# Routing of a mixture of experts inside an attention loop: its VectorE work moved between two other operations, its phases moved to other steps, shared batches started earlier

## The reference

```python
# x: (16, 256, 256), ctx: (16, 77, 256); 16 heads of 64
z = layernorm(x)
x = x + tanh(g_xattn) * cross_attention(keys_values=concat(LN(ctx), LN(z)), queries=LN(z)) @ Wo
h = layernorm(x)                       # 4096 rows of 256
logits = h @ router_w + router_bias    # 16 experts, the last one is the identity
top_w, top_i = top_k(softmax(logits), 2); w = top_w / sum
routed = w[15] * h + sum_e w[e] * (silu(h @ gate[e]) * (h @ up[e])) @ down[e]
shared = silu(causal_conv3(h)) * (h @ shared_up) @ shared_down
x = x + tanh(g_ffn) * (shared + routed)
```

## Time and profile before

| | |
|---|---|
| median of three runs | 1423.63 us (1422.02 to 1424.4) |
| profiled execution | 1424.07 us, its span 1422.3 us |
| busy: PE, DVE, ACT, POOL | 1267.8 (89%), 936.7 (66%), 636.0 (45%), 741.2 (52%) |
| mean granted TensorE clock | 0.984 |
| POOL per step | 0.74 us (L1094) and three times L1097 |

### The profile page before, as it was taken

One profiled execution on the slowest core, in us unless ns is written; L12 is line 12 of the kernel. 1 busy time (PEld: TensorE's weight loads), 2 busy tenths in 40 slices (PEclk: granted clock), 3 DMA queues, 4 the chain that ended last, 5 costly groups with the idle time before them and its releaser, 6 DMA issues.

```text
span 1422.3 us, 28174 instructions
## 1 busy us (share of the span) xinstructions
PE 1267.8 (89%) x8982; PEld 1020.6 (72%) x8982; DVE 936.7 (66%) x2710; ACT 636.0 (45%) x1956; POOL 741.2 (52%) x894
## 2 busy tenths in 40 slices
PE   1899999999998999899999998999999967998995
PEld 1677777777777777777777776777777755777774
DVE  4566676777776777677767776777776655445555
ACT  2554545454544454445444444444455412333332
POOL 1645546474656565556555655565554611444444
PEclk9999999999999999999999999999999989999998
DMA  4940000000000000000000000000000331335555
GB/s 129 310 122 4 3 1 18 1 19 1 18 1 20 2 18 8 13 6 14 9 13 9 11 9 13 9 11 9 9 12 5 94 104 41 105 118 167 177 171 189
DMA packets 61827, 70.94 MB, mean 50 GB/s; under 512 B 7056, under 2 KB 56160, under 8 KB 61664
## 3 DMA queue, kind: packets, MB, share of 16 engines
q1 hardware_dynamic: 54464, 49.96, 12.2%
q0 software_dynamic: 6912, 18.95, 3.6%
q10 hardware_dynamic: 288, 0.00, 0.0%
HBM read 35.19 MB, written 33.70 MB: 48 GB/s over the span
## 4 chain that ended last, share of the span: by engine, by line
PE 57%; DVE 21%; ACT 11%; issue 8%; DMA 2%; POOL 0%; DVEq 0%; SPq 0%; ACTq 0%; POOLq 0%
PE pj L1333 15%; PE st L1363 9%; ACT probs L1147 8%; PE st L1379 7%; PE ov L1398 5%; DVE neg_max L1286 5%; PE yb L1460 5%; PE st L539 4%; PE pj L492 3%; DVE OT_hl L1297 2%; PE ov L558 2%; ACT OT_hl L1155 1%; PE st L529 1%; DVE PT L1315 1%; PE ov L997 1%
## 5 line engine op out<-in xcount | busy, mean ns | idle before, releaser
L1097 POOL TENSOR_SCALAR probs<-probs,inv_sum 128x333 f32<-128x333 f32 x384 | 427.1, 1126 | 0.0
L1147 ACT ACTIVATE probs<-st,neg_max 128x333 f32<-128x333 f32 x512 | 268.8, 538 | 298.6 <-DVE neg_max L1286 298.6
L1094 POOL TENSOR_TENSOR probs<-probs,inv_sum 128x333 f32<-128x333 f32 x128 | 94.7, 740 | 457.0 <-DVE inv_sum L1293 457.0
L1286 DVE TENSOR_REDUCE neg_max<-st 128x2 f32<-128x666 f32 x256 | 205.9, 846 | 117.6 <-PE st L1379 115.0
L1363 PE MATMUL st<-ident,probs 128*128 128x128 f32 (+1 forms) x1536 | 206.7, 274 | 9.9 <-ACT probs L1147 9.9
L1363 PEld LDWEIGHTS st<-ident,probs 128*128 128x128 f32 (+1 forms) x1536 | 181.2, 145 | 28.9 <-ACT probs L1147 10.4
L1398 PE MATMUL ov<-PT,V 128*64 128x256 f32 (+1 forms) x1536 | 196.7, 391 | 0.1
L1333 PE MATMUL pj<-wkv,lT 128*128 128x512 f32 (+1 forms) x576 | 160.0, 414 | 28.8 <-DVE Q_hl L1302 28.6
L1315 DVE COPY PT<-st 128x512 f32<-128x512 f32 x256 | 164.3, 683 | 11.3 <-PE st L1363 9.8
L1379 PE MATMUL st<-K_hl,Q_hl 64*128 64x334 f32 x1536 | 153.1, 329 | 19.5 <-issue 8.0
L1379 PEld LDWEIGHTS st<-K_hl,Q_hl 64*128 64x128 f32 x1536 | 120.6, 187 | 41.5 <-issue 36.3
(11 more groups left out here) (175 smaller groups left out, 1815.3 us busy)
## 6 DMA issues: line engine op xcount, KB each, us to landing
slots_x<-zeros SPq DMA_DIRECT2D x10, 1032.0 KB, 13.2
V<-slots_x SPq DMA_DIRECT2D x80, 129.0 KB
yg<-routed_y SPq DMA_DIRECT2D x32, 256.0 KB, 3.1
out<-X SPq DMA_DIRECT2D x32, 128.0 KB
stage<-in_L_xattn_Wkv SPq DMA_DIRECT2D x4, 512.0 KB, 4.3
X<-in_x SPq DMA_DIRECT2D x2, 1024.0 KB, 14.6
w_gu<-in_L_ffn_expert_gate_w SPq DMA_DIRECT2D x2, 960.0 KB, 9.6
w_gu<-in_L_ffn_expert_up_w SPq DMA_DIRECT2D x2, 960.0 KB, 10.4
```

Source lines behind the costliest of these rows:

```text
L1094: pool.tensor_tensor(probs[:, v, 0, 0:SKV], probs[:, v, 0, 0:SKV], inv_sum[:, v, 0:1].to_broadcast([P, SKV]), ALU.mult).then_inc(normed, 1)
L1097: pool.tensor_scalar(probs[:, v, i, 0:SKV], probs[:, v, i, 0:SKV], inv_sum[:, v, i:i + 1], None, ALU.mult).then_inc(normed, 1)
L1147: nc.scalar.activation(probs[:, v, i, 0:SKV], st_bank(i)[:, 0:SKV], ACT.Exp, bias=neg_max[:, v, i:i + 1], accum_out=sums[:, v, i:i + 1]).t ...
L1286: nc.vector.tensor_reduce(neg_max[:, v, 2 * i:2 * i + 2], st[i][:, :, 0:SKV], AX.X, ALU.max, negate=True).then_inc(maxed, 1)
```

## The change

Routing phases get other steps and names: STATS 13, VAR 14, ROWS 16, TURN 17 and 18, LOGITS 19, PICK and RANK 22, PAGES 23, SLOTS (and the first scatter) 26, SECOND 27. So they fall on p = 5 (STATS), 6 (VAR, PICK, RANK), 7 (PAGES), 0 (ROWS), 1 and 2 (TURN), 2 (SLOTS), 3 (LOGITS, SECOND). `L_STEPS` moves from p = 3, 4 to 4, 5. On VectorE `route_vector` goes from the end of the step to the place between the maxima (and layer norm) and the reciprocal; `route_vector_reads` goes to the end. On TensorE `route_tensor` goes behind the transposes, ahead of the output projection; on ScalarE `route_scalar` goes to the end of the step.

Behind attention, the last steps of attention and routing (128 to 147) become items ("attend") of the written order, with nine shared items among them instead of seven, the first behind step 128. A shared item is split on VectorE: `shared` keeps the normalised rows of the batch after the next, `gate` has the rest and comes, among the tiles, one tile later. Shared items stand behind every eighth tile. The early `weights` cover 28 row tiles.

```diff
-    EARLY = 7
+    EARLY = 9
+    WEIGHED = QT * (B - 2)
...
+        steps = list(range(att.N, att.last_step + 1))
+        goes_along = (1, 1, 2, 1, 2, 2, 3, 4, 4)
         items = []
         for i in range(EARLY):
+            for _ in range(goes_along[i]):
+                items.append(("attend", steps.pop(0)))
+            if i == 2:
+                items.append(("weights", slice(0, WEIGHED)))
+            items += [("shared", i), ("gate", i)]
...
-            if i % 7 == 6 and shared < B + 2:
+            if i % 8 == 0 and EARLY + i // 8 == shared:
+                if i:
+                    items.append(("gate", shared - 1))
+            if i % 8 == 7 and shared < B + 2:
                 items.append(("shared", shared))
                 shared += 1
...
         def shared(i):
+            if i == 0:
+                dve.wait_ge(att.h_rows, B - 2)
+                rows(0)
+            if i + 1 < B:
+                rows(i + 1)
+
+        def gate(i):
             on = live(i, 3, B)
...
-    L_STEPS = {3: 0, 4: 1}
+    L_STEPS = {4: 0, 5: 1}
...
+    STATS, VAR, ROWS, TURN, LOGITS, PICK, RANK, PAGES, SLOTS, SECOND = 13, 14, 16, 17, 19, 22, 22, 23, 26, 27
...
@@ vector, step: between layer norm and the reciprocal
             if exists(b + 1) and exists(b) and p < 3:
                 layer_norm(b + 1, p)
+            route_vector(dve, bb, u, has)
             if has(LAG_S):
                 m, v = PAIRS * bb + u - LAG_S, (u - LAG_S) % 2
                 dve.wait_ge(exped, 4 * m + 4)
                 nc.vector.reciprocal(inv_sum[:, v, :], sums[:, v, :]).then_inc(inv_ready, 1)
...
-            route_vector_reads(dve, bb, u, has)
             next_rows = p in L_STEPS and exists(b + 1) and exists(b)
...
-            route_vector(dve, bb, u, has)
+            route_vector_reads(dve, bb, u, has)
...
@@ tensor, step: behind the transposes, ahead of the output projection
-            if (turns_conv or any(phase(bb, u, has, f) for f in (15, 16, 17, 19))) and has(LAG_AV):
-                pe.wait_ge(ot_lo, PAIRS * bb + u - LAG_AV + 1)
+            if has(LAG_Y):
+                pe.wait_ge(ot_lo, PAIRS * bb + u - LAG_Y + 1)
...
+            route_tensor(pe, bb, u, has)
             if has(LAG_Y):
```

More of the change, by code:

```diff
@@ L465, in combine, with tensor @@
                 add(t, 1).then_inc(final, 1)
-        follow(dve, att.route_vector, {"shared": shared, "weights": weights, "tile": tile, "sum": combine})
-    def tensor(pe):
+        follow(attend, {"shared": shared, "gate": gate, "weights": weights, "tile": tile, "sum": combine})
+    def tensor(pe, attend):
         for i, free in enumerate(att.pj_free):
@@ L716, in attention @@
     cv_full = sem("cv_full")
-    route_in = {f: sem(f"route_in{f}") for f in (12, 17, 18, 20, 21, 22)}
-    CHAIN = {12: 1, 17: 2, 18: 4, 20: 7, 21: 7, 22: 1}
+    STATS, VAR, ROWS, TURN, LOGITS, PICK, RANK, PAGES, SLOTS, SECOND = 13, 14, 16, 17, 19, 22, 22, 23, 26, 27
+    route_in = {f: sem(f"route_in{f}") for f in (STATS, LOGITS, PICK, PAGES, SLOTS, SECOND)}
+    CHAIN = {STATS: 1, LOGITS: 1, PICK: 6, PAGES: 7, SLOTS: 7, SECOND: 1}
     def fills(n):
@@ L814, in chain, with hold @@
             return then
-        def hold():
-            nc.vector.memset(route_carrier[:], 0.0)
-        at = phase(bb, u, has, 12)
+        def hold(i):
+            nc.vector.memset(route_carrier[:, i:i + 1], 0.0)
+        at = phase(bb, u, has, STATS)
         if at:
             j, v = at
-            then = chain(12, j)
+            then = chain(STATS, j)
             dve.wait_ge(y_read, j + 1)
-            hold()
+            hold(0)
             for t in range(QT):
@@ L831, in route_vector @@
             last.then_inc(h_var, 1)
-        at = phase(bb, u, has, 14)
+        at = phase(bb, u, has, ROWS)
         if at:
@@ L844, in route_vector @@
             nc.vector.tensor_copy(h_send[:, v, :, D], tiles_of(kept.row_id, j)).then_inc(h_rows, 1)
-        at = phase(bb, u, has, 17)
+        at = phase(bb, u, has, PICK)
         if at:
             j, v = at
-            then = chain(17, j)
-            dve.wait_ge(route_in[17], CHAIN[17] * j + 1)
-            hold()
+            then = chain(PICK, j)
+            dve.wait_ge(route_in[LOGITS], j + 1)
+            hold(1)
             for t in range(QT):
@@ L853, in route_vector @@
             then(last)
-            hold()
+            hold(1)
             for t in range(QT):
                 last = nc.vector.max_index(index[:, t, :], top[:, t, :], logit[:, t, :])
[L857 to L868, removed]
+            then(last)
             nc.vector.tensor_copy(tiles_of(kept.logits, j), logit[:])
@@ L909, in route_vector @@
             then(tt(base[:], base[:], grown[:, 3], ALU.add))
-        at = phase(bb, u, has, 23)
+        at = phase(bb, u, has, SECOND)
         if at:
@@ L918, in route_vector_reads @@
     def route_vector_reads(dve, bb, u, has):
-        at = phase(bb, u, has, 17)
+        at = phase(bb, u, has, LOGITS)
         if at:
@@ L924, in route_vector_reads @@
                                     kept.bias[:].unsqueeze(1).to_broadcast([P, QT, E]), ALU.add
-                                    ).then_inc(route_in[17], 1)
-        at = phase(bb, u, has, 19)
+                                    ).then_inc(route_in[LOGITS], 1)
+        at = phase(bb, u, has, RANK)
         if at:
@@ L957, in route_pool @@
                                ).then_inc(h_std, 1)
-        for i, f in enumerate((22, 23)):
+        for i, f in enumerate((SLOTS, SECOND)):
             at = phase(bb, u, has, f)
@@ L1183, in step @@
                 copy(PT[0:kn, v, 2, :], st_bank(2)[0:kn, :], ACT.Copy).then_inc(pt_hi, 1)
-        pipeline(act, step)
+            if isinstance(bb, int) and bb == 0 and 6 <= u < 6 + kept.KS_:
+                act.wait_ge(cv_full, u - 5)
+                copy(kept.w_cv[:, u - 6], H_COLS.rearrange("p (k i) -> p k i", k=KD), ACT.Copy
+                     ).then_inc(kept.cv_ready, 1)
+            route_scalar(act, bb, u, has)
+        return pipeline(act, step)
     def vector(dve):
```

155 lines of the change are left out of this document (61 added, 94 removed).

## The result

The changed kernel takes 1366.01 us, the median of 4 runs (1364.39 to 1368.16); the kernel before took 1423.11 us beside it (1422.02 to 1424.4). The ratio is 0.9596, interval 0.9581 to 0.9611: 57 us faster. The forecast was 1373. The profiled execution took 1364.59 us, 59.5 less than that of before, and its span is 1362.8 us.

What follows compares the result with a forecast made beforehand. It took routing queued ahead of VectorE's maxima (p = 5) and late reciprocals to slow steps TensorE otherwise paces. Loop 41.6 plus end 9 gave 50.6 us off the profiled 1424.07, which is 0.44 above the median: 1373, range 1352 to 1395.

Steps and rivals of the forecast that it cites:

- w + 3.75: Loop: length in us of a step with V projection, w being when VectorE's work before the reciprocal ends; at least 7.98.
- The first rival: Moved routing chains keep their high price between maxima and reciprocal: 1.5 us a batch, 21 us, 1394 us; chance 0.18.
- the hole: VectorE's wait of up to 1.5 us between maxima and reciprocal, for the exponentials, 141.5 us in all; the change fills it.
- 1.0 is passed on: Loop, p = 3: SECOND's wait for the first scatter delays the reciprocal and lengthens the step by 1.0 us, to about 7.9.
- The third rival: First scatter lands late, each us lengthening p = 3 by a us; up to 60 us, 1433 us; chance 0.04.
- The loop's sum: Attention loop: 2.98 us saved a batch, 38.7 over batches 2 to 14, with batches 1 and 15 41.6 us.
- The end's sum: Behind the loop: 17 us gained in the tiles less 8 in the stage before them, a gain of 9 us.
- I take + 8: Stage before the first tile: 8 us longer, for two more shared batches and the last batch's longer route.
- The second rival: Stage before the tiles, at TensorE's lower clock and waiting for VectorE, costs 17 more instead of 8: 1382 us; chance 0.08.
- my bound of 12 for that case: Tiles: 12 us gained if splitting the shared item saves no stall; 17 was the forecast, 24 with all saved.
- The range's lower end: Whole kernel: 1352 us, bounded by 24 gained in the tiles and both extra shared batches fully hidden before them.
- the low price in the hole: Moved routing chains run at their price with GpSimd idle, for example 0.41 instead of 0.62 us for a large ROWS operation.

Runs made afterwards that it cites:

- e6: Changed kernel with SLOTS moved to p = 4, SECOND to p = 6, and the last steps earlier among the shared items; 1355.48 us, ratio 0.9519.
- e5: Changed kernel with SECOND one step later, in p = 4 instead of p = 3; 1356.94 us, ratio 0.9527.
- e3: Changed kernel with seven shared items ahead of the tiles instead of nine, the others behind every seventh tile; 1375.27 us, ratio 0.9652.
- e9: Changed kernel with 26 unread transposes on TensorE ahead of the ranks of batches 14 and 15; 1361.83 us, ratio 0.9554.
- e1: Changed kernel with VectorE's routing work back at the end of the step, the new phases kept; 1431.69 us, ratio 1.004.
- e2: Kernel before, old phases kept, with VectorE's routing between layer norm and reciprocal and the logits' maxima one step later; 1413.97 us, ratio 0.9916.
- e7: Changed kernel with SECOND in p = 4 and the last steps regrouped, the last batch's routing one shared item earlier; 1353.08 us, ratio 0.9483.
- e8: Changed kernel with SLOTS in p = 4, SECOND in p = 6, and a shared item between each SLOTS and its SECOND behind the loop; 1350.17 us, ratio 0.9473.
- e10: The kernel of e8 plus the 26 unread transposes of e9 ahead of the last two batches' ranks; 1345.37 us, ratio 0.9458.

## Why the prediction was right, step by step

**The rule of the loop held.** w + 3.75 with w = 4.75 and 4.65 gave, with 0.1 for a turn and 0.5 for RANK, 8.60 and 8.90 for p = 2 and 6; measured 8.75 and 8.89, the reciprocals at 4.97 and 4.66. (Layer norm's 3.02 and SLOTS' 1.8 make 4.82 and not 4.75, which is a part of p = 2's miss.) p = 1 was 8.11 (8.18 predicted), p = 5 8.30 (8.28), p = 0 8.23 (8.40), p = 4 8.13 (8.28), p = 7 6.75 (6.96). e6 tried the rule three more times, to within 0.1 us. The first rival is refuted: L843 has a mean of 0.401 us, 0.614 before, never beside GpSimd's multiplications. ROWS as a whole costs 0.75 in the hole (the reciprocal of p = 0 is at 4.46, layer norm ends at 3.71), less than the 1.0 in the sum, although its two minima take only 0.42 off 1.66.

**The wait for the landing: right in time, too dear.** The timeline of VectorE in batch 10, p = 3, whose QK starts at 702.47:

```profile
703.54 1.60 DVE L1276 TENSOR_REDUCE neg_max<-st 128x2 f32<-128x666 f32 x2
707.24 0.17 DVE L904 TENSOR_SCALAR h_send<-h_send 128x2 f32<-128x2 f32 x1 [2.10 <-DMA slots_x<-h_send,slot_i]
...
707.50 0.18 DVE L1287 RECIPROCAL inv_sum<-sums 128x4 f32<-128x4 f32 x1
...
708.64 1.28 DVE L1308 COPY PT<-st 128x512 f32<-128x512 f32 x2
```

SECOND starts 4.8 into the step (4.9 predicted) and the reciprocal at 5.0 (5.2). But the step is 7.46 in the median and not 7.92. The step of the sum that failed is "1.0 is passed on": the PT copies end 7.45 into the step, and TensorE, with the logits and Y behind the transposes, is busy until 7.44 anyway. e5 has 7.32 without any wait. The wait costs 0.14 in the median and 3.1 us in all. The third rival, in which each us of it was a us of the step, was wrong from the first us for the same reason.

**The loop's sum was too small by 20 us.** 61.4 measured, 41.6 forecast. Of it, 11.3 is the steps' medians (3.85 a batch for 2.98, thirteen times: p = 3 0.46 better, p = 7, 0 and 4 0.15 to 0.21, p = 2 0.15 worse). 4.4 lies in batches longer than the medians, most of them at the ends of the rounds of the loop, before (mean 69.63, medians 68.50) as after (65.44, 64.65). 2.9 is batch 0, which I had left out altogether, 1.2 batches 1 and 15 and the start.

**The end's sum was too large by 11 us.** "I take + 8" for the stage was 16.2. Two more items are 6.4 of it (e3), and the other 9.8 is there with seven too, mostly as idle time. With nine it is busy time: TensorE idles as long as before (21.8 for 22.9), and its matmuls take 66.5 us for 49.2. The two items were priced at 4.9 each, which would make 59.0; e5 has 57.4 for the same matmuls, and its stage of 80.5 is the forecast's 80. So the term that was mis-sized is the price of the matmuls in the stage: the + 8 had a part for the two items and for the longer route, none for a lower clock, and at a granted 0.81 the matmuls took 7.5 us more than the 59.0 and 9.1 more than in e5. Filling two pauses took 6.3 off (e9), moving SECOND 7.8 (e5), both with shorter matmuls; the parts overlap and don't add up. SECOND's standing was priced at 1.0 a step in the loop, and cost 0.14 there; in the stage it cost some 1.5 directly, for batch 14 (e5). The second rival's mechanism, then, was half right: the lower clock is shown, but TensorE's idle time did not grow. Its size was right: the end cost 11 more than forecast, where that rival had 9 more. It didn't decide the time, because the loop gave more.

In the tiles a cycle of eight with one item is 19.11, so the item costs 19.11 - 8 x 1.63 = 6.07, as before (6.05). No idle time was saved by splitting it: the stall went to the tile behind the gate, 0.90 us for xT. The tiles gained 13.9, near my bound of 12 for that case, not 17.

The two errors, 20 too little and 11 too much, left 1364.6 for 1373. That the total came within 9 us of the forecast is partly luck: the loop's error alone would have left it 20 off and the end's 11, either of them still inside the range. The range's lower end doesn't follow from its own terms either: all of the idle time saved in the tiles would be 66.5 - 9 x 5.11, about 20 and not 24, and even with 24 the sum is 1358, not 1352.

**Shown and not shown.** Shown by runs: that the place and the rest of the loop's change work only together (e1, e2), nine against seven items (e3), what moving SECOND is worth (e5), SLOTS' place (e6), the clock (e9). Only argued, from one profile each: that e7 and e8 gain by covering batch 15's landing. Open: the new steps without TensorE's new order, the rest of what lengthens batches in e1, why e5's matmuls ran at a higher clock behind pauses of the same length, and why in e10 one pause was mended and the other not, beyond that it was longer.

## What to carry to other kernels

Work on an in-order engine is priced by where it stands: find the wait that ends the step, take the latest start that doesn't move it, and fill up to there; here the routing cost nothing up to 4.2 us into the step and one for one beyond. A wait for a transfer put into such an engine's order is cheap where another engine is as late anyway; it cost 0.14 us in a step in which the engine stood 2.1. Moving it a step behind the landing was still worth 9.1 us (e5), most of it in the stage behind the loop and through the length of matmuls, so look at all that a move changes. Price the drain behind a loop by its own timeline, with the clock: pauses of a few us on TensorE were paid a second time in the matmuls behind them.

## What the runs showed of the hardware

**The low clock shows behind a pause, at once or a us later.** In e8 the ranks right behind a pause of 3.64 us still took 0.41, and the conv one us later 4.38; in the changed kernel, behind 4.60 us, the ranks themselves took 0.64, and in e5, behind 4.59, they took 0.41 and the conv 3.88. A conv of 2.76 lost between 0.8 and 2.4 us to it. The Trainium skill (TensorE: Matmul & The Clock Gate, The HAM clock gate) says that the low level is the state of an array without activity and that activity lifts it; the trace agrees, with 0.64 against 0.41 for the same ranks, and e9 adds that activity whose result nobody reads does as well.

**Running beside GpSimd doesn't by itself make a VectorE operation dear.** The copy `best<-top` in the timelines of VectorE, first the kernel before, then e1; GpSimd's three multiplications ran from 598.07 to 601.42 and from 766.50 to 769.81:

```profile
599.90 0.43 DVE L870 COPY best<-top 128x4 f32 x1
```

```profile
769.18 0.16 DVE L862 COPY best<-top 128x4 f32 x1
```

The same operation beside the same work costs 0.43 in one and 0.16 in the other. It is so in each of the 14 batches whose copy stands beside the multiplications: 0.41 to 0.44 in the kernel before, 0.16 in e1. Of the two large operations of ROWS, both 0.60 to 0.68 beside GpSimd before, e1 has one at 0.41 and the other at 0.55 in most batches, beside GpSimd again. What decides it, these runs don't show; the low price in the hole, used in the forecast, held.
